# Top-64 attention stages: the order of TensorE's output sums, and added idle products

## The reference, cut to what matters

```python
scores = jnp.einsum('bhqd,bhkd->bhqk', qh, kh) / np.sqrt(DHEAD)
vals, idx = jax.lax.top_k(scores, 64)
scores = jnp.full_like(scores, neg).at[bI, hI, qI, idx].set(vals)
probs = jax.nn.softmax(scores, axis=-1)
ctx = jnp.einsum('bhqk,bhkd->bhqd', probs, vh)
x = _layernorm(x + ctx @ wo_w.T + wo_b)
```

## Time and profile before

| | us |
|---|---|
| median of 3 runs | 9845.44 (9834.27 to 9868.88) |
| the profiled execution | 9871.3 |
| its span, first to last instruction | 9869.5 |
| top-64 stage l0xc in it | about 1270 to 3876 |
| top-64 stage l1ac in it | about 4825 to 7640 |
| mean granted TensorE clock | 0.703 |
| DVE busy / PE busy | 6915.2 (70%) / 7384.9 (75%) |
| ACT busy / POOL busy | 4440.3 (45%) / 3933.2 (40%) |

### The profile page before, as it was taken

The page is one execution under the profiler, slowest core; times in us unless marked ns, Lnnn a source line. Parts: engine busy times, 40 slices in busy tenths (PEclk is TensorE's granted clock), DMA queues, the critical chain, the costliest instruction groups (busy, mean ns, idle before and its releaser), DMA issues. The chain is left out here.

```text
span 9869.5 us, 164232 instructions
## 1 busy us (share of the span) xinstructions
PE 7384.9 (75%) x30924; PEld 2873.3 (29%) x30924; DVE 6915.2 (70%) x47725; ACT 4440.3 (45%) x8379; POOL 3933.2 (40%) x2613
## 2 busy tenths in 40 slices
PE   6888557766666656999677777767767889999983
PEld 2222222222222223565222222222223422222222
DVE  2655289999999996455599999999997243343323
ACT  1444145556565554111466666656656422222220
POOL 1000044445444443122255555545544035555550
PEclk7888655555555556899665655556655899999986
DMA  2000200000000000000100000000000311111103
GB/s 59 22 23 18 45 7 7 7 4 7 4 7 4 7 4 2 26 19 6 36 5 8 4 8 4 8 4 4 8 4 2 134 39 38 31 28 38 31 16 81
DMA packets 85578, 199.43 MB, mean 20 GB/s; under 512 B 25265, under 2 KB 39599, under 8 KB 80815
## 3 DMA queue, kind: packets, MB, share of 16 engines
q1 hardware_dynamic: 73390, 174.17, 6.5%
q10 hardware_dynamic: 11264, 16.79, 0.7%
HBM read 123.17 MB, written 66.95 MB: 19 GB/s over the span
## 5 line engine op out<-in xcount | busy, mean ns | idle before, releaser
L2097 DVE TENSOR_REDUCE l1xc_part_max<-l1xc_by_query 128x1 f32<-128x512 f32 (+1 forms) x1024 | 558.2, 571 | 898.1 <-PE l1xc_by_query L1956 881.8
L768 DVE MAX8 l1ac_cand<-l1ac_score 128x8 f32<-128x32 f32 x8192 | 957.3, 185 | 50.9 <-ACT l1ac_score L675 25.1
L2055 ACT ACTIVATE l1xc_prob<-l1xc_less_max 128x512 f32<-128x512 f32 (+1 forms) x832 | 451.2, 594 | 1147.8 <-PE l1xc_less_max L1970 982.2
L768 DVE MAX8 l1ac_cand<-keep_xT 128x8 f32<-128x32 f32 x8192 | 953.9, 184 | 4.4
L768 DVE MAX8 l0xc_cand<-l0xc_score 128x8 f32<-128x25 f32 (+1 forms) x8192 | 894.4, 176 | 43.7 <-ACT l0xc_score L675 29.1
L550 POOL TENSOR_SCALAR l1ac_lost<-l1ac_score,l1ac_tops 128x2048 bf16<-128x2048 f32 x128 | 695.6, 5434 | 527.6 <-DVE l1ac_tops L787 484.8
L703 ACT ACTIVATE l1ac_prob<-l1ac_less_max 128x512 f32<-128x512 f32 x1024 | 602.3, 592 | 665.2 <-PE l1ac_less_max L596 661.3
L768 DVE MAX8 l0xc_cand<-keep_xT 128x8 f32<-128x25 f32 (+1 forms) x8192 | 896.2, 177 | 4.4
L550 POOL TENSOR_SCALAR l1ac_lost<-keep_xT,l1ac_tops 128x2048 bf16<-128x2048 f32 x128 | 695.9, 5437 | 365.3 <-DVE l1ac_tops L787 365.3
L1918 POOL TENSOR_TENSOR l1xc_total<-l1xc_total,l1xc_prob 128x2048 f32<-128x2048 f32 (+1 forms) x176 | 793.9, 4511 | 71.7 <-POOL l1xc_v_tile L1928 71.4
L703 ACT ACTIVATE l0xc_prob<-l0xc_less_max 128x512 f32<-128x512 f32 (+1 forms) x832 | 489.0, 592 | 648.7 <-PE l0xc_less_max L596 647.9
(11 more groups left out here) (461 smaller groups left out, 15142.9 us busy)
## 6 DMA issues: line engine op xcount, KB each, us to landing
l1xc_k<-wide_k SPq DMA_DIRECT2D x32, 400.2 KB, 5.2
moe_w<-in_L_ffn_mlp_w_dram SPq DMA_DIRECT2D x16, 512.0 KB, 4.1
wide_q<-l1xp_full SPq DMA_DIRECT2D x8, 1024.0 KB, 3.9
wide_q_parts<-l1xp_parts SPq DMA_DIRECT2D x16, 512.0 KB, 5.6
l1xc_q_hm<-wide_q_parts SPq DMA_DIRECT2D x32, 256.0 KB, 3.8
l1xc_q<-wide_q SPq DMA_DIRECT2D x32, 256.0 KB, 5.6
wide_sums<-l1xc_o_out ACTq DMA_DIRECT2D x64, 128.0 KB, 2.3
l1xf_num<-wide_sums SPq DMA_DIRECT2D x16, 512.0 KB, 11.5
```

The source lines that it names most:

```text
L768: seg = nc.vector.max(new[:, j:8 * NSEG:NSEG], score[i % 4][:, a:a + w])
L2055: nc.scalar.activation(prob[0:n, buf(j), c], yP[c % 2][0:n], ACT.Exp).then_inc(y_taken, 1)
L2097: nc.vector.tensor_reduce(part_max[:, i % 2, c:c + 1], a_bank(i, c)[:, 0:w], AX.X, ALU.max).then_inc(a_taken, 1)
```

## The change

1. TensorE's slot: the output sums of the quad before move from ahead of unit 0 to behind unit 1; unit 2 moves from behind flag and turn to ahead of them. New order: search, units 0 and 1, sums, unit 2, flag (turn), combine, unit 3.
2. ScalarE's slot: `take_sums` moves from ahead of exponential 0 to behind exponential 1, ahead of the flag's copy.
3. Each unit begins with idle products: 4, 2, 4 or 8 products of the bf16 identity with a 128x512 tile of ones, into the bank that the unit then fills from scratch. They stand behind the wait for the bank and ahead of the waits for masks, checks and statistics.
4. GpSimd fills the tile of ones (`warm`) once per stage.

```diff
+        warm = s.sb("warm", [P, CH], BF16)
...
-        READY = 6
+        READY = 7
+        WARM = (4, 2, 4, 8)
...
+            nc.gpsimd.tensor_copy(warm[:], G.ones[:]).then_inc(ready, 1)
...
                 hold(pe, (y_taken, UNITS * h + y_freed(c, j) + Y_AHEAD))
+                for _ in range(WARM[j % 4]):
+                    nc.tensor.matmul(bank[:], G.identb[:], warm[:], start=True, stop=True, skip_group_check=True)
                 if j == 0:
...
-                if exists(h, i):
-                    sums(hq, cq, kq)
                 todo = []
...
                 for x in todo[0:2]:
                     unit(*x)
+                if exists(h, i):
+                    sums(hq, cq, kq)
+                for x in todo[2:3]:
+                    unit(*x)
                 if settles(h, i):
                     it = (i - SET) % QT
                     flag(h * QT + i - SET, it, 4 * hq + cq if exists(h, i) else 0)
                     if it % 4 == 3:
                         turn(h if i >= SET else h - 1, it // 4)
-                for x in todo[2:3]:
-                    unit(*x)
                 if ending:
                     combine(hq, cq, h * QT + i - SET + 1 if settles(h, i) else H * QT)
...
-                if ending:
-                    take_sums(*quad_before(h, i)[0:2])
                 todo = []
...
                 for x in todo[1:2]:
                     weigh(*x)
+                if ending:
+                    take_sums(*quad_before(h, i)[0:2])
                 if settles(h, i):
                     flag(h * QT + i - SET, it)
```

## The result

| | before | after |
|---|---|---|
| median of 20 runs, us | 9845.44 (9820.32 to 9890.16) | 9879.86 (9826.71 to 9894.17) |
| the profiled execution, us | 9871.3 | 9876.18 |
| mean granted TensorE clock | 0.703 | 0.886 |
| TensorE busy, us | 7384.9 | 7990.8 |
| instructions | 164232 | 180866 |

The ratio is 1.0028 [1.0017, 1.004]: slower by 0.3%, where 0.7% faster was forecast. The 9880 us lie just above the top of the range, 9875.

The account below looks back on a forecast made before the run. VectorE's top-64 search was taken as the bound, TensorE counting only where VectorE waits for the flag. L1 -77, L0 0 and tails +10 gave -67 us: 9804 profiled, 9778 for the median, range 9670 to 9875.

Parts of the forecast that it names:

- number 4: L0 at the loop jump: ending slot, ScalarE's stand and next flag take 21.7 us against 20.8, +14 us in all.
- the -14 inside the heads: L0, behind ending slots within a head: flag after 17.9 us against 18.4, so 14 us less waiting.
- a bound of +170: Slow bound of L0's term, the flag late behind cold idle products: +170 us, beside a fast bound of -57.
- Number 3: Sums behind units 0 and 1, both queues: ordinary L1 slot's flag at 6.4 us, slot end 8.9, full clock.
- Step 2: TensorE's clock rises but falls in half of L1's slots, 3 to 4 us at half clock; L0's ending slots start cold.
- Step 4, L1: L1's waits for the flag: -60 us mainly inside heads, -7 at jumps, -10 from an earlier start, together -77.
- Step 5: Stage tails, where nothing hides idle products: +5 us a stage, +10 together; GpSimd's copy into `warm` taken at 0.
- Rival 3: Flag late behind cold idle products, mainly in L0's ending slots and their successors: slower, about 9980 us; chance 0.12.
- Rival 2: Waits inside heads go (-74), those at the jumps grow (+54), tails +10: about 9835 us; chance 0.17.
- Rival 1: Clock holds nearly always, flag at 6.4 us: L1 -125, L0 -57, tails +10, giving 9673 us; chance 0.20.
- Rival 4: Idle products don't raise the clock, TensorE becomes the bound in both stages: +1460, about 11300 us; chance 0.03.

## Why the prediction was wrong

- **What bounds the kernel**: right. VectorE's tiles without a wait kept 9.9 to 10.1 us in L1 and 9.4 to 9.7 in L0 in every kernel but the one with the old order and idle products. What can be won is its waits: 186.6 us, and the order alone won 175 in the two stages. Not all of VectorE's waits stand ahead of L789: some 1.7 us a head in L0 stand ahead of its search (L768), at its own loop jump, before as well as with the sums moved.
- **The failed step is number 4, its L0 term at the jump**: 12.0 + 2.4 + 7.3 = 21.7 us against 20.8, so +0.9 a jump and, with the -14 inside the heads, 0 for the stage. Measured: 14.0 + 4.3 + 8.1 = 26.4 against 20.7, so +5.7 a jump, and +83 for the stage. The 14 jump tiles grew by 60 us in all, the 14 tiles ahead of them by 20 (11.1 us against 9.7), and everything else by 3. Three terms were too small. The stand was taken as before, with nothing for a fetch of TensorE's loop: it grew by 2.1 us, and the instructions added to the body had stood in the diff with no row of their own. Slot 15 with its cold idle products takes 14.0 us and lies above the prediction's own 10.5 to 13.1. The next slot's flag comes after 8.1 us in place of 7.3. That L0 comes out at 0 was the difference of two small terms, +14 and -14, with a bound of +170 beside it.
- **Number 3**, the price of the new order: its numbers for L1 came, the comparison beside them is missing. It worked out the flag at 6.4 us against 8.0, and the slot at 8.9 against 9.8, for the full clock with idle products. Measured: 6.3 and 9.0. The new order at half clock without idle products was never priced. From the same rows it is 8.0 less the sums' 1.87 us that no longer stand ahead of exponential 0, so 6.1; measured 6.1. So the prediction could not see that one part of the change held all of the gain and the other only cost.
- **Step 2**, the clock: forecast 0.85 to 0.95 in L1 (0.94) and 0.75 to 0.85 in L0 (0.87). Mechanism right, size of the falls somewhat too large: a fall in half of the L1 slots was taken, and the clock stayed through the idle time in nearly all. In L0 nearly every ending slot started cold, as forecast (57 of 60, 0.51 in the first 2 us).
- **Step 4, L1**: -77 forecast, -82 measured, -11 of it in the jump tiles. The sum at the jump came too: 21.5 us forecast, 21.6 measured (11.0 + 2.5 + 8.1). What the number hides is that the order gives -124 and the idle products take +42.
- **Step 5**: the tails +10 forecast, about +15 measured; the copy into `warm` 0 to 1 us, 0.61 us measured on GpSimd (the run with idle products only before the jump).
- **Rivals.** Rival 3 had the right mechanism, the flag behind cold idle products, but placed it behind every ending slot (48 x 2.6 us). It acts at the jumps. Inside L0's heads the ending slot starts cold too, but its successor is at full clock again: 12.2 + 6.1 = 18.3 us to the flag (medians), as much as before. Rival 2 (given inside the heads, taken at the jumps) is nearest to what came, 9835 against 9880. It fits L0's jumps, where its 1.8 us a jump was too small; in L1 the jump tile became shorter, 13.5 to 12.9 us. Rival 1 came true for the clock and not for the time, and its -125 us in L1 is more than the 121.7 us of waits from which it is taken. Rival 4 falls: the Trainium skill's "TensorE: Matmul & The Clock Gate", Part 4: PE-mode transpose, speaks of products in transpose mode; ordinary products against an identity raised the clock of L1 from 0.69 (new order alone) to 0.94.
- **What stays open.** Both stages fetch as much (137 and 138 packets), but TensorE stalls 3.9 to 4.9 us a jump in L0 and 0.9 to 3.0 in L1. Why is not shown; the shorter stall, beside ScalarE's own stand, is what makes it cheap there. Nor is it shown why slot 15 takes 14.0 us when the other ending slots of L0, which start cold too, take 12.2 (median).

The version that beats both kernels is the one with the sums moved and no idle products: 9676.6 us, 1.8% under before. The new order alone gives the same within the intervals.

## What to carry to other kernels

Price each part of a change by itself, at the clock that it would have alone; the part without cost may hold all of the gain. A higher TensorE clock is worth only what the engine that sets the end waits for TensorE: here moving 1.9 us of sums out of the ring left hardly any such wait, and the clock was then worth nothing. Filler has two prices that its busy time doesn't show: in these runs it ran at half clock just behind the idle time, at the seams of the loop, and it lengthens the loop body, so read the instruction queue's bytes beside the clock.

## What the runs showed of the hardware

- A TensorE loop body longer by 232 products a head in L0 (464 instructions, since each has its load of weights) stalls 3.9 to 4.9 us at each of 14 jumps; with 196 products more (the run without them in the two slots at the jump) it stalls at one jump of 14. The change from one to the other is sharp, but the number of instructions alone does not set it. With 1738 recorded TensorE instructions a head, L1 of the run with idle products ahead of units 0 to 2 fetches nothing anew, L1 of the fp32 run does at each jump (137 packets), and L0 of the full change does with 1697.
- An fp32 product of 512 columns stands in the trace as two matmul instructions and takes 1.87 us at half clock (2198.44 to 2200.31), where four bf16 products take 1.68 (2213.80 to 2215.48 in the kernel after). So a clock as high (0.902 against 0.886) came from 173319 instructions in place of 180866.
- ScalarE stands 2.2 to 2.4 us at its own loop jump, mostly with nothing to wait for in the profile (2.44 before, 2.16 with fp32 idle products). TensorE's stall in L1 lies beside it and cost 0.2 us a jump with one-column products.
- Products that nobody reads, ordinary ones against an identity, raised the granted clock from 0.62 to 0.87 in L0 and from 0.69 to 0.94 in L1, against the new order alone. In L0 of the run with them ahead of unit 3 only, idle times of TensorE of 4.0 to 4.7 us (means by slot) stand behind the slots with a single unit, and the next slot began at 0.50 in all 60 cases.
